# A decoder layer on one core: cross-attention's transposes go from TensorE to the DMA queue, its output projection a quarter later

## The chip, the core and the metric

The kernel is one program on one core of a Trainium2 chip. The metric is the device time of one execution in microseconds (us), lower is better. The numbers compared are medians of several executions.

## The reference

Three blocks follow one another over `x` of 4 x 2048 x 512, each with a residual and a layer normalisation: a self-attention sum, cross-attention, and a feed-forward block with 16-bit and 8-bit rounding. The change touches the second only. With 16 heads of 32, 154 keys and a bias for each head, query and key, it is

```
q, k, v = split_heads(x1), split_heads(ctx), split_heads(ctx)      # 4 x 16 x (2048 or 154) x 32
weights = softmax((q @ k.T + bias) / sqrt(32))                     # bias 1 x 16 x 2048 x 154
combined = merge_heads(weights @ v)                                # 4 x 2048 x 512
x2 = layernorm(x1 + combined @ w_out)
```

## The kernel before

`cross_attention_stage` cuts the queries into 16 units of 512 tokens (the four batches in turn at one position, then the next position: four units are a span, `s`, and the unit's batch is `b`). A unit has four quarters. Quarter `q` = 4n + i does several things side by side, each for another tile: with 128 tokens a tile, with four heads a group. Every engine has its own `quarter` function that lists its work in order, and `at(n, i, off)` (for SP and POOL `span_at`) says for which tile or group: `off` quarters ahead of q or behind it. Engines wait for each other by counting semaphores alone.

The steps, with the offset in quarters before the change:

- SP loads the tile's x1 (`load_x1`, +4). ACT rounds it to f16 as `q16` (`token_half`, +5); the same pair of x1 and q16 gives the f16 stack: the rounded q twice (`stack_halves`, +5) and, from POOL, the rest that rounding lost (`low_half`, +4). A head of the stack has 97 columns: high, high, low, and one for minus its maximum.
- PE transposes q16 into PSUM (`transpose_heads`, line 1161, 4 transposes of 128x128), ACT copies it to `q_heads` (line 977). PE multiplies it with the keys and adds the bias rows (`max_pair`, +4, 16 matmuls of 308 columns), and DVE takes each head's maximum into the stack (`maximum`, line 1041).
- PE transposes the stack, 16 heads in two halves (`transpose_stack`, line 1192, +4 and +3), ACT copies it to `qs` (line 986).
- `logits` (+0): 5 steps for the group's four heads, keys on the partitions. DVE adds the bias (`add_bias`, line 1054), ACT takes the exponential (`weights`, line 996). `values` (-1) are 20 products in f32, `normalise` (-1, -2) divides by the sum.
- The combined group is split into f16 high (ACT, `combined_high`, -2) and low (POOL, `combined_low`, -2), transposed by PE (`transpose_combined`, line 1249, 8 transposes, -3) and copied by ACT to `combT` (line 1013).
- `project` (-6): 12 matmuls of 512 columns for one tile, then DVE's `residual` (-6), POOL's `reciprocal_root` and `finish` (-7), with the store, and DVE's `magnitude` (-8).

All transposes on PE share one bank of PSUM, `ps_t16`, so each waits until ACT has copied the one before. Inside a PE quarter there are eight slots k: in each `max_pair`, in the first five `logits`, 2 or 3 of `values`, in the odd ones a quarter of `project`; the transposes stand in slots 0, 2, 4 and 6.

SP issues all loads of the stage in one queue, in order. Keys and values of the next batch come once a unit, the bias in `bt_main` and `bt_tail` (1.25 MB for each group) four times a span: in the last three quarters of it and the first of the next. POOL loads `b_rows` (616 KB a tile slot) four times a span from its own queue: before the change at b = 2, i = 1 to 3 and b = 3, i = 0. PE, ACT and DVE loop over 8 quarters a turn, SP and POOL over 16.

The feed-forward stage already uses a DMA transpose (line 1407, `xT`): 128 x 2048 f16, 512 KB, twice for each of its 16 blocks, in a stage that loads and stores blocks of 1 MB.

Of the kernel before, what the change touches and what calls it, by code (L numbers as in the profile page):

```python
# [37 lines left out]
SPAD = STACK + 1  # L38
# [586 lines left out]
def cross_attention_stage(nc, x1_rows, ks_dram, kb_dram, v_main, v_tail, bias_rows, bias_main, bias_tail,  # L625
# [12 lines left out]
    with ExitStack() as ctx:  # L638
# [49 lines left out]
        ps_t = ctx.enter_context(nc.psum_tensor("ps_t", [P, 512], F32))  # L688
        ps_t16 = ps_t[:, :].bitcast(F16)
# [17 lines left out]
        qT_done = sem("qT_done")  # L707
        qT_ready = sem("qT_ready")
        mx_done = sem("mx_done")
        mx_ready = sem("mx_ready")  # L710
        st_done = sem("st_done")
        st_ready = sem("st_ready")
# [9 lines left out]
        ct_done = sem("ct_done")  # L722
        ct_ready = sem("ct_ready")
# [22 lines left out]
        def over_quarters(eng, quarter):  # L746


            for q in range(-5, 16):
# [5 lines left out]
            for q in range(QUARTERS - 8, QUARTERS + 9):  # L755
                quarter(q // 4, q % 4, (q // 4) % 2)

        def over_spans(eng, quarter):

            for q in range(-5, 16):  # L760
                quarter(q // 16, q // 4 % 4, q % 4)
# [4 lines left out]
            for q in range(QUARTERS - 16, QUARTERS + 9):  # L766
                quarter(q // 16, q // 4 % 4, q % 4)
# [13 lines left out]
        def _(sp):  # L781
            def load_x1(s, b, t):
# [9 lines left out]
            def load_residual(s, b, t):  # L792
# [3 lines left out]
                if not (isinstance(s, int) and tile < 2):  # L796
                    sp.wait_ge(y_ready, tile - 1)
                first_tile = 4 * s if isinstance(s, int) else sp.snap(4 * s)
                sp.dma_start(xres[:, t % 2], x1_rows[b].rearrange("(n p) d -> n p d", p=P)[
                    bass.ds(first_tile + t, 1)].rearrange("n p d -> p (n d)")).then_inc(xres_in[t % 2], 16)  # L800
# [31 lines left out]
            def quarter(s, b, i):  # L832
                n = 4 * s + b if isinstance(s, int) else sp.snap(4 * s + b)
                if isinstance(s, int) and n < 0:
# [21 lines left out]
                if not (isinstance(s, int) and s == UNITS // BATCH - 1) and b == BATCH - 1 and i >= 1:  # L856
                    sp.wait_ge(biased, 5 * (4 * n + i))
                    load_bias(s + 1 if isinstance(s, int) else sp.snap(s + 1), i - 1)
# [4 lines left out]
            over_spans(sp, quarter)  # L863

        @block.gpsimd
        def _(pool):
# [7 lines left out]
            def low_half(s, b, t):  # L874
# [4 lines left out]
                if not (isinstance(tile, int) and tile < 2):  # L879
                    pool.wait_ge(st_done, 2 * (tile - 1))  # L880
# [4 lines left out]
            def combined_low(s, b, g):  # L885
# [4 lines left out]
                if not (isinstance(group, int) and group == 0):  # L890
                    pool.wait_ge(ct_done, group)
                pool.tensor_tensor(comb_lo[:], comb[:], comb_hi[:], ALU.subtract).then_inc(comb_split, 1)  # L892
# [54 lines left out]
        def _(act):  # L947
            def token_half(nu, t):
# [5 lines left out]
                if not (isinstance(tile, int) and tile < 2):  # L954
                    act.wait_ge(qT_done, tile - 1)
# [3 lines left out]
            def stack_halves(nu, t):  # L959
# [4 lines left out]
                if not (isinstance(tile, int) and tile < 2):  # L964
                    act.wait_ge(st_done, 2 * (tile - 1))
# [3 lines left out]

            def copy_heads(nu, t):  # L970
                if not inside(nu, t):
                    return
                tile = 4 * nu + t
                act.wait_ge(qT_done, tile + 1)
                if not (isinstance(tile, int) and tile < 2):
                    act.wait_ge(mx_done, 8 * (tile - 1))
                act.activation(q_heads[:, t % 2], ps_t16[:, 0:DIM], ACT.Copy).then_inc(qT_ready, 1)

            def copy_stack(nu, t, eu, half):
                if not inside(nu, t):  # L980
                    return
                tile = 4 * nu + t
                act.wait_ge(st_done, 2 * tile + half + 1)
                if not (isinstance(nu, int) and nu < 2):
                    act.wait_ge(lg_done, 20 * (nu - 1))
                act.activation(qs[:, eu, 8 * half:8 * half + 8, t * P:(t + 1) * P],  # L986
                               ps_t16[0:STACK, :].rearrange("p (h t) -> p h t", t=P), ACT.Copy).then_inc(st_ready, 1)
# [10 lines left out]
            def combined_high(nu, g):  # L998
# [4 lines left out]
                if not (isinstance(group, int) and group == 0):  # L1003
                    act.wait_ge(ct_done, group)
                act.activation(comb_hi[:], comb[:], ACT.Copy).then_inc(comb_high, 1)  # L1005

            def copy_combined(nu, g, eu):
                if not inside(nu, g):
                    return
                act.wait_ge(ct_done, 4 * nu + g + 1)  # L1010
                if not (isinstance(nu, int) and nu < 2):
                    act.wait_ge(w_done, 4 * (nu - 1))
# [1016 lines left out]
```

## Time and profile before

| | |
|---|---|
| Median of 3 runs | 2423.58 us (2409.52 to 2452.31) |
| The profiled execution | 2424.86 us |
| Its span, first to last instruction | 2423.3 us |
| PE busy | 2182.9 us, 90% |
| DVE busy | 1762.9 us, 73% |
| ACT busy | 1235.8 us, 51% |
| POOL busy | 819.8 us, 34% |
| Mean granted TensorE clock | 0.948 of full speed |
| Mean moved by the DMA engines | 168 GB/s |

Cross-attention lies between about 565 and 1425 us of the span. A time "busy" counts an engine's instructions only; a matmul's end is modelled, so that matmuls that follow one another overlap on paper, and the distance between starts tells more than their lengths.

### The profile page before, as it was taken

What the parts mean: (1) busy time and instruction counts of PE and PEld (TensorE: products, weight loads), DVE (VectorE), ACT (ScalarE), POOL (GpSimd) and SP (SyncE); (2) the same over time, 40 slices, a digit from 0 to 9 for tenths busy, and PEclk for the clock granted to TensorE, in tenths of its full rate; (3) what the DMA queues carried; (4) which work ended last, traced back from release to release, by engine and by line L of the source; (5) the groups of instructions that cost most, each with busy time, mean ns of one, the idle gap of its engine ahead of it and who ended that gap; (6) DMA issues with size and microseconds to landing.
All of it is one profiled execution on the core that took longest, in us unless ns stands there. A gap on an engine that the chain in (4) does not pass through costs nothing. (4 is left out here: it accounts for less than half of the span.)

```text
span 2423.3 us, 40289 instructions
## 1 busy us (share of the span) xinstructions
PE 2182.9 (90%) x13184; PEld 1238.5 (51%) x13184; DVE 1762.9 (73%) x3344; ACT 1235.8 (51%) x1714; POOL 819.8 (34%) x819
## 2 busy tenths in 40 slices
PE   7998999973999999999899937899999959999998
PEld 3444444431777777777677713334444424444443
DVE  5768687853787878687778835886666468888885
ACT  1444444443776766576567504344444455555551
POOL 2212222221144445344445444123222214433442
PEclk9999999996999999899989978999999979999999
DMA  6334332228437338334723136777888746666662
GB/s 219 119 103 144 116 130 103 102 81 185 131 95 186 126 109 173 125 102 102 198 96 105 57 133 214 266 231 256 266 274 268 282 157 232 229 224 226 231 228 84
DMA packets 219008, 406.52 MB, mean 168 GB/s; under 512 B 111526, under 2 KB 111814, under 8 KB 200416
## 3 DMA queue, kind: packets, MB, share of 16 engines
q1 hardware_dynamic: 154800, 244.18, 32.8%
q0 software_dynamic: 64048, 160.28, 20.0%
q8 instruction: 91, 1.49, 0.3%
q14 instruction: 69, 0.57, 0.1%
HBM read 259.00 MB, written 138.73 MB: 164 GB/s over the span
## 5 line engine op out<-in xcount | busy, mean ns | idle before, releaser
L1680 PE MATMUL ps_h<-xT,w 128*128 128x512 f16 x2048 | 453.1, 384 | 22.0 <-ACT h L1511 12.2
L1920 PE MATMUL ps<-w,g_hi 128*128 128x512 f16 x1024 | 389.7, 381 | 28.3 <-DVE g_lo L1858 28.3
L1920 PE MATMUL ps<-w,g_lo 128*128 128x512 f16 x1024 | 389.6, 380 | 0.0
L1041 DVE TENSOR_REDUCE stack<-ps_m 128x2 f16<-128x308 f32 x512 | 244.7, 480 | 133.8 <-PE ps_m L1178 109.8
L1680 PEld LDWEIGHTS ps_h<-xT,w 128*128 128x128 f16 x2048 | 201.1, 99 | 268.2 <-issue 19.3
L1511 ACT ACTIVATE h<-ps_h,b_in_sb,col_scale 128x512 f32<-128x512 f32 x256 | 198.0, 778 | 261.3 <-PE ps_h L1680 230.1
L1236 PEld LDWEIGHTS ps_o<-vm,pT 128*128 128x128 f32 x2048 | 292.0, 198 | 12.9
L1236 PE MATMUL ps_o<-vm,pT 128*128 128x33 f32 x2048 | 278.5, 261 | 0.0
L1587 DVE TENSOR_REDUCE amax_t<-h 128x1 f32<-128x2048 f32 x64 | 146.2, 2284 | 128.7 <-ACT h L1511 128.1
L996 ACT ACTIVATE pT<-logit 128x512 f32<-128x512 f32 x320 | 198.8, 624 | 71.3 <-DVE logit L1054 70.6
L1806 ACT ACTIVATE g_hi<-g 128x2048 f16<-128x2048 f32 x64 | 122.2, 1909 | 176.1 <-DVE g L1849 153.0
L297 ACT ACTIVATE raw<-ps_proj 128x512 bf16<-128x512 f32 x128 | 76.4, 597 | 249.9 <-PE ps_proj L563 249.9
L892 POOL TENSOR_TENSOR comb_lo<-comb,comb_hi 128x512 f16<-128x512 f32 x64 | 74.2, 1160 | 380.7 <-ACT comb_hi L1005 380.7
L1773 POOL TENSOR_TENSOR rstd<-vare,minus_half 128x1 f32<-128x1 f32 x64 | 132.1, 2064 | 189.2 <-DVE vare L1876 189.2
L1176 PE MATMUL ps_m<-kb,q_heads 128*128 128x308 f16 x512 | 156.4, 306 | 32.1 <-DMA b_rows<-bias_rows 13.4
L1920 PEld LDWEIGHTS ps<-w,g_hi 128*128 128x128 f16 x1024 | 100.5, 98 | 151.9 <-DVE g_lo L1858 30.6
L1054 DVE TENSOR_TENSOR logit<-ps_l,bt_main 128x512 f32<-128x512 f32 x256 | 173.8, 680 | 1.6 <-PE ps_l L1214 1.6
L1920 PEld LDWEIGHTS ps<-w,g_lo 128*128 128x128 f16 x1024 | 100.5, 98 | 121.1 <-issue 1.4
L1264 PE MATMUL ps_w<-wo_hi,combT 128*128 128x512 f16 x512 | 156.8, 389 | 5.1 <-DVE y L1082 3.1
L1178 PE MATMUL ps_m<-b_rows,ident_h 128*128 128x308 f16 x512 | 156.1, 305 | 0.0
L563 PE MATMUL ps_proj<-x_hi,w_hi 128*128 128x512 f16 x512 | 136.3, 390 | 17.2 <-DVE x_lo L383 17.2
L986 ACT ACTIVATE qs<-ps_t 97x1024 f16<-97x1024 f16 x128 | 129.7, 1013 | 40.5 <-PE ps_t L1192 39.9
(180 smaller groups left out, 4149.1 us busy)
## 6 DMA issues: line engine op xcount, KB each, us to landing
hidden<-h POOLq DMA_DIRECT2D x64, 1024.0 KB, 6.0
hT<-hidden SPq DMA_DIRECT2D x64, 1024.0 KB, 6.3
xc<-x_cols SPq DMA_DIRECT2D x16, 1024.0 KB, 5.3
xr<-x_rows SPq DMA_DIRECT2D x16, 1024.0 KB, 5.7
x_rows<-x POOLq DMA_DIRECT2D x16, 1024.0 KB, 4.8
x1t<-x_rows SPq DMA_DIRECT2D x64, 256.0 KB, 5.2
bt_main<-bias_main SPq DMA_DIRECT2D x16, 1024.0 KB, 7.6
xres<-x_rows SPq DMA_DIRECT2D x64, 256.0 KB, 3.6
```

What stands on the lines that cost most here:

```text
L563: mm = pe.matmul(ps_proj[job % 2][:], w[:, m, c, o * P:(o + 1) * P], x_[:, j % 2, c, :], start=(s == 0), stop=(s == len(terms) - 1))
L996: act.activation(pT[:, g % 2, k, :], logit[:, (g + k) % 4], ACT.Exp, scale=SCALE).then_inc(exp_done, 1)
L1041: dve.tensor_reduce(stack[:, t % 2, 2 * k:2 * k + 2, 3 * HD], ps_m[k % 2][:, 0:2 * KEYS].rearrange("p (h k) -> p h k", h=2), AX.X, ALU.max ...
L1054: dve.tensor_tensor(logit[:, (g + k) % 4], ps_l[(5 * g + k) % 2][:], bias, ALU.add).then_inc(biased, 1)
L1176: pe.matmul(out, q_heads[:, t % 2, (k // 2) * P:(k // 2 + 1) * P], kb[:, eu, 2 * k * KEYS:(2 * k + 2) * KEYS], start=True, stop=False)
L1178: pe.matmul(out, ident_h[:], b_rows[:, t, 2 * k:2 * k + 2, :], start=False, stop=True).then_inc(mx_done, 1)
L1236: mm = pe.matmul(ps_o[c][:, base + h * VW:base + (h + 1) * VW], pT[:, g % 2, part, tok], vm[:, eu, 4 * g + h, :], start=False, stop=(part ...
L1264: mm = pe.matmul(ps_w[:], combT[:, eu, a, c, t * P:(t + 1) * P], w[:, c, :], start=(c == 0 and a == 0 and w is wo_hi), stop=(c == KC - 1 a ...
L1511: act.activation(h[:, f // 4, f % 4, :], ps_h[f % 4][:], ACT.Gelu, bias=b_in_sb[:, f:f + 1], scale=col_scale[:, f:f + 1]).then_inc(h_ready, 1)
L1587: dve.tensor_reduce(amax_t[:], h[:, g].rearrange("p c t -> p (c t)"), AX.X, ALU.max, apply_absolute_value=True).then_inc(h_max, 1)
L1680: mm = pe.matmul(ps_h[f % 4][:], w1[:, c, f * P:(f + 1) * P], xT[:, e, a, :, c, :], start=(a == 0 and c == 0), stop=(a == 1 and c == KC - 1))
L1920: mm = pe.matmul(ps[t][:], g[:, e, f, t * P:(t + 1) * P], w2[:, f, :], start=(f == 0 and a == 0), stop=(f == FC - 1 and a == 1))
```

## The change

The three transposes are issued by SP as DMA transposes, straight into `q_heads`, `qs` and `combT`; the 28 transposes on PE and the four copies on ACT in each quarter go, and with them the PSUM bank `ps_t`. A head in the stack is padded from 98 to 128 columns, so that one DMA transposes 16 blocks; `qs` has 128 rows, of which `logits` uses 97. The two halves of the combined heads lie in one double-buffered `comb_parts`. The offsets move: `load_x1` +4 to +7, `token_half` +5 to +7, `stack_halves` +5 to +6, `low_half` +4 to +6, `max_pair` and `maximum` +4 to +5, `project` and `residual` -6 to -7, `finish` -7 to -8, `magnitude` -8 to -9. The rows of `b_rows` are loaded in all four quarters of b = 2. The loops run from quarter -8 and a quarter longer, and SP's is written out in full, without a loop on the chip.

```
@@ buffers
-        stack = sb("stack", [P, 2, HEADS, SPAD], F16)
+        stack = sb("stack", [P, 2, HEADS, P], F16)
-        qs = sb("qs", [STACK, 2, HEADS, BLK], F16)
+        qs = sb("qs", [P, 2, HEADS, BLK], F16)
-        comb_hi = sb("comb_hi", [P, 2, 2, P], F16)
-        comb_lo = sb("comb_lo", [P, 2, 2, P], F16)
-        combT = sb("combT", [P, 2, 2, KC, BLK], F16)
+        comb_parts = sb("comb_parts", [P, 2, 2, 4, P], F16)
+        combT = sb("combT", [P, 2, KC, 2, BLK], F16)
@@ sync (SP)
+            def turn_heads(s, b, t):
...
+                sp.wait_ge(q16_ready, tile + 1)
+                if tile >= 2:
+                    sp.wait_ge(mx_done, 8 * (tile - 1))
+                sp.dma_start_transpose(q_heads[:, t % 2].rearrange("p (c r) -> p c r", r=P),
+                                       q16[:, t % 2]).then_inc(qT_in[t % 2], 16)
+
+            def turn_stack(s, b, t):
...
+                sp.wait_ge(mx_ready, 8 * (tile + 1))
+                sp.wait_ge(high_ready, tile + 1)
+                sp.wait_ge(low_ready, tile + 1)
+                if n >= 2:
+                    sp.wait_ge(lg_done, 20 * (n - 1))
+                sp.dma_start_transpose(qs[:, n % 2, :, t * P:(t + 1) * P],
+                                       stack[:, t % 2].rearrange("p h d -> p (h d)")).then_inc(st_in[t % 2], 16)
+
+            def turn_combined(s, b, g):
...
+                sp.wait_ge(comb_split, 4 * n + g + 1)
+                if n >= 2:
+                    sp.wait_ge(w_done, 4 * (n - 1))
+                sp.dma_start_transpose(combT[:, n % 2, g].rearrange("p a (t r) -> p (a t) r", r=P),
+                                       comb_parts[:, g % 2].rearrange("p a t d -> p (a t d)")).then_inc(ct_in[g % 2], 16)
@@ SP's quarter
-                load_x1(*span_at(s, b, i, 4))
-                load_residual(*span_at(s, b, i, -6))
+                turn_heads(*span_at(s, b, i, 6))
+                turn_stack(*span_at(s, b, i, 4))
+                if 4 * n + i >= -3:
+                    load_x1(*span_at(s, b, i, 7))
+                if n < 0:
+                    return
+                turn_combined(*span_at(s, b, i, -3))
+                load_residual(*span_at(s, b, i, -7))
...
-            over_spans(sp, quarter)
+            for q in range(-8, QUARTERS + 10):
+                quarter(q // 16, q // 4 % 4, q % 4)
@@ POOL's quarter
-                low_half(*span_at(s, b, i, 4))
                 combined_low(*span_at(s, b, i, -2))
-                reciprocal_root(*span_at(s, b, i, -7))
-                finish(*span_at(s, b, i, -7))
+                reciprocal_root(*span_at(s, b, i, -8))
+                finish(*span_at(s, b, i, -8))
+                low_half(*span_at(s, b, i, 6))
...
-                elif b == 2 and i >= 1:
-                    pool.wait_ge(mx_done, 8 * (4 * (n + 1) + i))
-                    load_rows(s + 1, i - 1)
-                elif b == 3 and i == 0:
-                    pool.wait_ge(mx_done, 32 * (n + 1))
-                    load_rows(s + 1, 3)
+                elif b == 2:
+                    pool.wait_ge(mx_done, 8 * (4 * (n + 1) + i + 1))
+                    load_rows(s + 1, i)
@@ ACT: stack_halves (tile >= 2)
-                    act.wait_ge(st_done, 2 * (tile - 1))
+                    act.wait_ge(st_in[t % 2], 16 * (2 * nu + t // 2))
@@ ACT's quarter
-                copy_combined(*at(n, i, -3), (e + (i - 3) // 4) % 2)
                 weights(n, i, 0)
                 weights(n, i, 1)
-                copy_stack(*at(n, i, 3), (e + (i + 3) // 4) % 2, 1)
                 weights(n, i, 2)
                 combined_high(*at(n, i, -2))
                 weights(n, i, 3)
-                token_half(*at(n, i, 5))
-                copy_stack(n + 1, i, 1 - e, 0)
+                stack_halves(*at(n, i, 6))
                 weights(n, i, 4)
-                copy_heads(*at(n, i, 5))
-                stack_halves(*at(n, i, 5))
+                token_half(*at(n, i, 7))
@@ PE: logits and project
-                    pe.wait_ge(st_ready, 8 * n + 7)
+                    pe.wait_ge(st_in[0], 32 * (n + 1))
+                    pe.wait_ge(st_in[1], 32 * (n + 1))
...
-                    pe.wait_ge(ct_ready, 4 * (nu + 1))
+                    pe.wait_ge(ct_in[0], 32 * (nu + 1))
+                    pe.wait_ge(ct_in[1], 32 * (nu + 1))
@@ PE's quarter
-                tile = (*at(n, i, -6), (e + (i - 6) // 4) % 2)
+                tile = (*at(n, i, -7), (e + (i - 7) // 4) % 2)
                 for k in range(8):
-                    max_pair(n + 1, i, 1 - e, k)
+                    max_pair(*at(n, i, 5), (e + (i + 5) // 4) % 2, k)
...
-                        transpose_combined(*at(n, i, -3), last_use)
-                        transpose_stack(*at(n, i, 3), 1,
-                                        (ct_ready, q - 2) if inside(*at(n, i, -3)) else (qT_ready, q + 5))
-                        transpose_stack(n + 1, i, 0, (st_ready, 2 * q + 8) if inside(*at(n, i, 3)) else (qT_ready, 1))
-                        transpose_heads(*at(n, i, 5))
```

## Rows read from the trace of the kernel before

**Rows 1.** Windows over cross-attention: length, busy time (instructions) by engine, clock, DMA share, GB/s.

```profile
565.70:609.05 43.35, 19.58 (x148) 10.35 (x149) 15.25 (x35) 18.03 (x27) 10.41 (x9) 0.72 1.09 236
609.05:795.62 186.57, 175.75 (x1550) 140.52 (x1549) 146.51 (x337) 131.75 (x205) 70.48 (x70) 0.95 0.51 137
795.62:1003.92 208.30, 196.65 (x1669) 151.78 (x1668) 162.47 (x385) 135.69 (x209) 96.92 (x100) 0.95 0.51 141
1003.92:1215.55 211.63, 200.03 (x1664) 154.11 (x1664) 162.77 (x385) 135.47 (x208) 96.89 (x100) 0.93 0.47 130
1215.55:1382.00 166.45, 165.76 (x1426) 129.99 (x1426) 136.35 (x330) 112.96 (x173) 80.07 (x85) 0.97 0.25 84
1382.00:1424.70 42.70, 30.58 (x205) 19.12 (x204) 26.51 (x73) 8.77 (x12) 31.90 (x37) 0.98 0.26 87
```

**Rows 2.** Windows over single quarters (from one `bt_tail` add of DVE to the next).

```profile
853.71:865.19 11.48, 11.48 (x105) 9.10 (x103) 10.04 (x25) 8.42 (x14) 5.76 (x6) 1.00 0.44 154
...
917.85:929.39 11.54, 11.54 (x105) 9.10 (x104) 9.95 (x26) 8.45 (x13) 6.96 (x8) 1.00 0.78 128
929.39:942.41 13.02, 12.16 (x108) 9.16 (x105) 11.65 (x26) 8.45 (x13) 7.67 (x8) 1.00 0.87 173
...
953.95:969.72 15.77, 12.36 (x93) 9.02 (x92) 9.92 (x26) 7.54 (x12) 6.48 (x7) 0.86 1.17 310
...
985.36:1003.92 18.56, 15.33 (x108) 10.84 (x105) 10.15 (x25) 8.51 (x14) 5.76 (x6) 0.79 0.49 166
1003.92:1019.74 15.82, 15.67 (x104) 11.97 (x104) 10.11 (x26) 8.56 (x13) 5.75 (x6) 0.71 0.22 67
```

**Rows 3.** Timeline of PE in one quarter: start, length, line, how many.

```profile
901.32 0.39 PE L1161 MATMUL ps_t<-ident_h,q 128*128 128x128 f16 x4
901.54 0.29 PE L1176 MATMUL ps_m<-kb,q_heads 128*128 128x308 f16 x1
...
904.20 0.39 PE L1249 MATMUL ps_t<-ident_h,comb_hi 128*128 128x128 f16 x4
...
904.65 0.29 PE L1176 MATMUL ps_m<-kb,q_heads 128*128 128x308 f16 x1
...
907.48 0.63 PE L1192 MATMUL ps_t<-ident_h,stack 128*97 128x128 f16 x8
907.95 0.29 PE L1176 MATMUL ps_m<-kb,q_heads 128*128 128x308 f16 x1
```

**Rows 4.** Waits from 640 to 1382 us: total, times, longest.

```profile
DVE stack L1041 <- PE ps_m L1178: 75.3, 144, 5.7
ACT q L957 <- DMA x1t<-x_rows: 15.4, 4, 6.2
```

**Rows 5.** Line 1407 by source, the feed-forward stage's DMA transposes: issue on SP min/median/max, and landing.

```profile
L1407 SPq DMA_TRANSPOSE xT<-x_hi x16: 1838/8844/9410, 1461.6 to 1882.6; - x16
L1407 SPq DMA_TRANSPOSE xT<-x_lo x16: 2137/6224/10310, 1463.9 to 1884.4; - x16
DMA to landing us min/median/max: 4.4/9.8/16.3
```

**Rows 6.** Window of one us in which only those transposes move data.

```profile
1531.00:1532.00 1.00, 0.00 (x0) 0.00 (x0) 0.86 (x3) 0.47 (x1) 0.00 (x0) 0.50 1.19 220
```

**Rows 7.** DMA issues from 800 to 1000 us: size, median us to landing.

```profile
x1t<-x_rows SPq DMA_DIRECT2D x16, 256.0 KB, 5.1
b_rows<-bias_rows POOLq DMA_DIRECT2D x4, 616.0 KB, 8.6
```

**Rows 8.** Timeline of ACT: two neighbouring tiles before the first logits; then two steady operations.

```profile
595.53 0.60 ACT L977 ACTIVATE q_heads<-ps_t 128x512 f16<-128x512 f16 x1 [0.56 <-PE ps_t L1161]
...
601.53 0.60 ACT L977 ACTIVATE q_heads<-ps_t 128x512 f16<-128x512 f16 x1 [0.56 <-PE ps_t L1161]
...
883.24 0.62 ACT L996 ACTIVATE pT<-logit 128x512 f32<-128x512 f32 x1
885.00 0.62 ACT L967 ACTIVATE stack<-x1t 128x512 f16<-128x512 f32 x1
```

More of the change, by code:

```diff
@@ L746, in over_quarters @@
         def over_quarters(eng, quarter):
-            for q in range(-5, 16):
+            for q in range(-8, 16):
                 quarter(q // 4, q % 4, (q // 4) % 2)
@@ L754, in over_quarters @@
                         quarter(2 * m + e, i, e)
-            for q in range(QUARTERS - 8, QUARTERS + 9):
+            for q in range(QUARTERS - 8, QUARTERS + 10):
                 quarter(q // 4, q % 4, (q // 4) % 2)
         def over_spans(eng, quarter):
-            for q in range(-5, 16):
+            for q in range(-8, 16):
                 quarter(q // 16, q // 4 % 4, q % 4)
@@ L765, in over_spans @@
                         quarter(s, b, i)
-            for q in range(QUARTERS - 16, QUARTERS + 9):
+            for q in range(QUARTERS - 16, QUARTERS + 10):
                 quarter(q // 16, q // 4 % 4, q % 4)
@@ L968, in stack_halves @@
                 act.activation(stack[:, t % 2, :, HD:2 * HD], x, ACT.Copy).then_inc(high_ready, 1)
[L970 to L987, printed above, removed]
             def weights(n, g, k):
@@ L1095, in _ @@
             dve.tensor_copy(ident_h[:], ident_f[:]).then_inc(ident_ready, 1)
+            dve.memset(stack[:, :, :, STACK:P], 0.0).then_inc(ident_ready, 1)
             def magnitude(nu, t):
@@ L1139, in quarter @@
                     if k == 7:
-                        residual(*at(n, i, -6))
+                        residual(*at(n, i, -7))
                     if k == 5:
@@ L1151, in _ @@
         def _(pe):
-            def transpose_heads(nu, t):
-                if not inside(nu, t):
-                    return
-                tile = 4 * nu + t
-                pe.wait_ge(q16_ready, tile + 1)
-                if not (isinstance(tile, int) and tile == 0):
-                    pe.wait_ge(st_ready, 2 * tile - 1)
-                for c in range(KC):
-                    mm = pe.transpose(ps_t16[:, c * P:(c + 1) * P], q16[:, t % 2, c * P:(c + 1) * P], ident_h[:])
-                mm.then_inc(qT_done, 1)
             def max_pair(nu, t, eu, k):
@@ L1179, in max_pair @@
                           start=False, stop=True).then_inc(mx_done, 1)
-            def transpose_stack(nu, t, half, last_use):
-                if not inside(nu, t):
-                    return
-                tile = 4 * nu + t
-                if half == 0:
-                    pe.wait_ge(high_ready, tile + 1)
-                    pe.wait_ge(low_ready, tile + 1)
-                pe.wait_ge(mx_ready, 8 * tile + 4 * half + 4)
-                pe.wait_ge(*last_use)
-                for h in range(8):
-                    mm = pe.transpose(ps_t16[0:STACK, h * P:(h + 1) * P],
-                                      stack[:, t % 2, 8 * half + h, 0:STACK], ident_h[:])
-                mm.then_inc(st_done, 1)
             def logits(n, e, g, k):
@@ L1240, in values @@
                         mm.then_inc(pv_done, 1)
-            def transpose_combined(nu, g, last_use):
-                if not inside(nu, g):
-                    return
-                pe.wait_ge(comb_split, 4 * nu + g + 1)
-                pe.wait_ge(*last_use)
-                for a, half in enumerate((comb_hi, comb_lo)):
-                    for t in range(4):
-                        mm = pe.transpose(ps_t16[:, (4 * a + t) * P:(4 * a + t + 1) * P], half[:, t // 2, t % 2, :],
-                                          ident_h[:])
-                mm.then_inc(ct_done, 1)
             def project(nu, t, eu, c):
```

88 lines of the change are left out of this document (37 added, 51 removed).

## The prediction

> **What bounds the kernel now.** I read the windows over the stage first, then single quarters, then PE's timeline in one of them, then waits and DMA. Cross-attention holds 859 us of the span, 64 quarters of logits between a lead-in of 43 us and a drain of 43 us [rows 1]. A quarter that nothing disturbs takes 11.5 us, PE is busy in all of it at a full clock, DVE for 10.04 us, and DMA for a share of 0.44 [rows 2]. So PE bounds it, and DVE is only 1.5 us behind. 16 quarters of 11.5 us would be 184 us, but the two middle spans take 208.3 and 211.6 [rows 1]: some 25 us of each go elsewhere. The single quarters show where: those with `b_rows` under way take 11.5 and 13.0 us at a DMA share of 0.78 to 0.87, the one with bias loads 15.8 at 1.17, and the ones after it 18.6 and 15.8 at a granted clock of 0.79 and 0.71, which is a mix of 2.4 and 1.2 GHz [rows 2]. Late x1 is among the causes there [rows 4].
>
> **Removed: PE's transposes.** Their cost is the distance between starts. Eight of the stack take 907.48 to 907.95, 0.47 us, twice a quarter; the eight of the combined heads 904.20 to 904.65, 0.45; the four of q16 901.32 to 901.54, 0.22 [rows 3]. That is 1.61 us of each quarter, and PE would need 9.9. But DVE has 10.04 of work, which the change leaves alone. Between PE and DVE stand two banks for the maxima and two for the logits, so DVE can't run far ahead, and some small waits stay. The bound is 10.04 below, 11.5 above; I take 10.5, nearer to the busy row, since DVE's present waits for PE (75 us in 742, 1.2 a quarter [rows 4]) come from PE being late. **A clean quarter gains 1.0 us, not 1.6.** ACT loses four copies and has slack before and after (8.42 of 11.5 [rows 2]); I cost that at nothing.
>
> **Added: DMA transposes.** In a quarter they move 128 + 512 + 256 KB (q16 512, stack 2048, combined 1024 columns of f16 on 128 partitions), 0.92 MB. While only `xT`'s transposes run, 220 GB/s go at a share above 1, that is, the engines are full [rows 6]: 4.2 us a quarter. The clean quarter's DMA work is 0.44 x 11.5 = 5.1 us at most, so 9.3 of 10.5: it fits, barely. A span has 0.51 x 208 = 106 us of it now [rows 1] and will have 106 + 67 = 173 in some 195: it fits too, if it is spread. It isn't.
>
> The Trainium skill (DMA: Bandwidth & Descriptors, "Latency and other measured facts") gives a contiguous DMA transpose 350 to 400 GB/s and says that a non-contiguous middle dimension costs about 30%. No row here has the first figure; `xT`'s target is contiguous and got 220. As an estimate by that page's 30%, the stack's transpose, whose heads lie 1 KB apart in `qs`, would take 1 us more, which would change the `b_rows` quarters below by 12 us in all and the clean ones by nothing.
>
> **The new loop.** SP issues in order: `turn_heads`, `turn_stack`, x1, `turn_combined`, the residual, then the keys, values or bias of the quarter. ACT's `stack_halves` of tile q+6 waits until the stack of q+4 has been read out, which SP issued at the start of the same quarter; behind it stand `weights` 4 and `token_half`, whose q16 the next `turn_heads` wants, and behind that is the next `turn_stack`. So a quarter can't be shorter than: the stack's issue to landing, plus two halves of 0.62, one exponential of 0.62 and one token half of about 0.62 [rows 8], plus SP's issue of the heads (a quarter of the 1.84 that 512 KB cost it [rows 5], 0.46) and their own 0.6 us of DMA. With the shortest landing, 4.4 us [rows 5], that is 7.9; with the median of 9.8, which was measured beside 1 MB stores, 13.3. In a clean quarter the ring holds little else, and x1 lands in 5.1 [rows 7] where it could be some 3; I take 4.4 + 2 = 6.4 and get 9.9, under DVE's 10.5. This is the step with the least room.
>
> **Quarters with b_rows** (12 of them, b = 2 in three spans; all now in a row). Their DMA share of 0.78 to 0.87 is 9.0 to 11.3 us of work [rows 2]; with 4.2 more it is 13.2 to 15.5. The rows aren't wanted for three quarters, so some of it can slip into b = 3, but their packets come from POOL's queue between those of the transposes and slow the stack's. I take 13.2 against 12.3 now: 12 x 0.9 = +11. Bounds: 10.5 (-22) and 15.5 (+38).
>
> **Quarters with bias, and after** (12). Bias loads stand behind the transposes in SP's queue, x1 has less than a quarter to arrive instead of two, so the late x1 stays. What shrinks is PE's work at a low clock: 1.6 of 11.5 is 14%, of 15.8 it is 2.2. I take -1.6 each, -19. Bounds: -3 and +2 each, -36 and +24.
>
> **Clean quarters.** The first six have no projection and are bound otherwise (I give them nothing); 58 - 24 = 34 remain: -34. Bounds: -1.46 each (-50) and +1.8 (+61, if the loop takes 13.3).
>
> **Lead-in.** Two tiles now follow at 6.0 us [rows 8], and logits start after four tiles. They will start after five and the landing of tile 3's stack; a tile takes the loop's 7.3 (no exponential yet). Four steps of 7.3 and about 5 of landing are 34 against 25, and the first heads queue behind the first loads, during which 236 GB/s flow at a share of 1.09 [rows 1]. For that I take 6, an estimate between nothing and 15: +9 and +6, +15 in all. Bounds 0 and +30.
>
> **Drain.** The last group's transpose costs 0.45 on PE and a copy of 1.02 now, and by DMA some 3.5 to landing (4.4 for twice as much, less half its 2.4 of transfer, plus issue); the quarter added behind holds only a projection: +4. Bounds 0 and +8. SP's three issues are 1.84 us for 512 KB [rows 5], so 3.2 for the quarter's 896 KB, and fit into 10.5 as long as the ring takes them. The padding's one memset and the merging of the combined halves lie on no chain, and POOL has 5.76 of 11.5 busy [rows 2], so that its later `low_half` fits.
>
> **Sum:** -34 + 11 - 19 + 15 + 4 = -23 us. Against the profiled execution of 2424.9 (1.6 us over its span) that is 2402. The median, 2423.6, lies 1.3 under that execution; I leave the number at 2402.
>
> **Rivals.**
>
> A. The forecast, chance 0.44: 2360 to 2450 with its own bounds.
>
> B. DMA hides everything, DVE is the bound throughout. For it: the mean share after, 173 in 195, is under 1, and the stalls by late x1 might be absorbed by the deeper pipeline. Against it: SP's order puts x1 behind 0.64 MB. Clean quarters -1.3 x 34, `b_rows` -1.8 x 12, bias -2.5 x 12, +11 at the ends: -85, 2340. Chance 0.27.
>
> C. The loop decides: the stack's landing takes more than 7 us in ordinary quarters, from where the loop passes 10.5. For it: the median landing of 9.8; SP was held 8.8 us by one issue [rows 5], so its queue itself stalls when the ring is full. Against it: those stand behind 1 MB loads and beside 1 MB stores, here 256 KB is usual. At a landing of 8.8 the quarter is 12.3: +0.8 x 34 = +27, `b_rows` at 15.5 +38, bias 0, ends +25: +90, 2515. Chance 0.27.
>
> D. The transposes don't overlap at all: each of the three waits out a landing of 4.4 one after another, 13.2 us a quarter, 1.7 more in 58 quarters and 25 at the ends: 2549. Rows 5 and 6 speak against it, since hi and lo of `xT` are both issued before the first lands. The Trainium skill (VectorE: DVE Perf Modes, "The three transpose paths") has a 128x128 block at 1309 ns by DMA against 390 on TensorE; 28 in a row would be 37 us a quarter by that. The row has 220 GB/s, 0.15 us for a block of 32 KB, and excludes it. Chance 0.02.
>
> **Numbers.** A measurement of this kernel can tell about 2% from no change: 48 us, so faster is under 2375, slower over 2472. A gives 0.03 faster, 0.40 same, 0.01 slower; B 0.22 and 0.05; C 0.04 same and 0.23 slower; D slower. Together 0.25, 0.49, 0.26. The range is 2335 to 2500: it leaves out half of C, D and the far end of B.
>
> **What would show it.** Right: clean quarters of 10.4 to 10.7 us with DVE busy for about 10 and PE idle in short pieces; quarters with b = 2 at 12.5 to 14 with a DMA share near 1; the stack's landing at 6 to 7 us, longer in those; first logits some 15 us later. Wrong: ACT's `stack` (line of `stack_halves`) waiting for the DMA transpose in clean quarters means C; PE at a lower clock in clean quarters, because it now waits briefly each time, would spoil A and B alike and is in no row here, since DVE-bound quarters with projection don't occur.

## The result, and the profile after

The changed kernel is slower, by 1.4%. Its median is 2461.28 us (4 runs, 2452.13 to 2478.65) against 2430.22 for the kernel before on the same chip (4 runs, 2409.52 to 2452.31): a ratio of 1.0142 [1.0101, 1.0183]. The forecast was 2402. The profiled executions, 2463.74 and 2424.86 us, lie 38.9 apart, and the 38.9 are what has to be found.

From the page of the kernel after: busy time, the granted clock in 40 slices, and the queues (packets, MB, share of 16 engines' span).

```profile
span 2462.2 us, 35958 instructions
PE 2154.9 (88%) x11368; PEld 1165.3 (47%) x11392; DVE 1775.3 (72%) x3345; ACT 1019.0 (41%) x1458; POOL 805.7 (33%) x819
...
PEclk9999999985558998989889977999999989999999
...
DMA packets 454485, 464.55 MB, mean 189 GB/s; under 512 B 347046, under 2 KB 347334, under 8 KB 435936
...
q1 hardware_dynamic: 390320, 302.92, 46.9%
```

ACT lost 217 us of work. PE lost only 28 us of busy time though 1792 transposes (28 x 64) left it: three slices of the stage stand at 5 tenths, that is, at a granted clock of 1.2 GHz, and there the rest of PE's work takes longer.

The windows over the stage after, with the columns of [rows 1]: lead-in, three spans, the last span, drain.

```profile
561.80:624.96 63.16, 23.44 (x87) 6.32 (x88) 20.25 (x44) 9.71 (x18) 11.07 (x10) 0.55 0.99 194
624.96:836.81 211.85, 195.64 (x1108) 146.95 (x1107) 144.43 (x330) 82.42 (x144) 67.23 (x67) 0.72 0.88 186
836.81:1043.35 206.54, 180.88 (x1216) 126.99 (x1216) 164.99 (x386) 81.02 (x144) 96.55 (x100) 0.91 0.97 209
1043.35:1251.62 208.27, 182.41 (x1216) 127.90 (x1216) 167.11 (x385) 80.80 (x144) 96.55 (x100) 0.89 0.90 201
1251.62:1410.98 159.36, 152.88 (x1071) 108.98 (x1072) 138.95 (x329) 66.92 (x119) 80.16 (x85) 0.95 0.69 165
1410.98:1456.00 45.02, 31.04 (x168) 17.08 (x166) 27.61 (x76) 4.68 (x8) 34.68 (x40) 0.92 0.42 120
```

The first span lost 25 us to [rows 1], at a clock of 0.72 against 0.95. The two middle spans gained 2 and 3, the last 7. The DMA share of the middle spans went from 0.51 and 0.47 to 0.97 and 0.90.

The single quarters of the kernel after, against [rows 2]: one before the projection starts; the first with b = 2, at whose end POOL issues `b_rows`, and the one behind it; one behind the boundary of a loop; two clean ones; one of the last span.

```profile
689.35:703.32 13.97, 13.97 (x65) 11.47 (x65) 8.18 (x18) 5.22 (x9) 2.27 (x2) 0.50 0.66 160
734.12:744.12 10.00, 10.00 (x78) 7.41 (x76) 8.98 (x23) 5.01 (x9) 5.04 (x6) 1.00 0.84 193
744.12:759.68 15.56, 11.54 (x80) 7.64 (x77) 9.59 (x25) 5.12 (x9) 8.86 (x9) 0.87 1.16 213
1043.35:1060.39 17.04, 16.90 (x73) 11.86 (x74) 10.04 (x25) 5.12 (x9) 5.74 (x6) 0.53 0.61 182
1071.71:1083.26 11.55, 10.40 (x76) 7.29 (x76) 11.02 (x25) 5.01 (x9) 5.74 (x6) 1.00 0.65 152
1083.26:1094.57 11.31, 10.40 (x76) 7.29 (x76) 10.59 (x26) 5.01 (x9) 5.74 (x6) 1.00 0.63 147
1290.58:1301.54 10.96, 10.40 (x76) 7.29 (x76) 10.24 (x25) 5.01 (x9) 5.74 (x6) 1.00 0.77 156
```

And the kernel before: the quarter that answers to the first of them (no projection either), ahead of it a stretch of its second quarter in which its clock was low too.

```profile
617.00:627.00 10.00, 10.00 (x56) 8.67 (x54) 5.02 (x9) 4.31 (x7) 1.16 (x1) 0.50 0.69 229
650.81:660.24 9.43, 9.10 (x93) 8.06 (x94) 7.54 (x18) 8.23 (x14) 2.27 (x2) 1.00 0.24 93
```

Cut at the same places in both kernels (from one `bt_tail` add to the next), the difference falls into these groups of quarters. The forecast's terms stand beside them.

| | before | after | difference | forecast |
|---|---|---|---|---|
| start to first logits | 609.05 | 624.96 | +15.9 | +15 |
| first eight quarters | 85.4 | 109.2 | **+23.8** | 0 (for six) |
| 12 of b = 2, `b_rows` | 147.9 | 162.3 | +14.5 | +11 |
| 12 with bias, and after | 185.0 | 165.4 | -19.6 | -19 |
| 28 clean | 314.6 | 307.0 | **-7.6** | -34 (for 34) |
| 3 at the end of a turn of the loop of PE, ACT and DVE | 42.1 | 42.2 | +0.1 | (in the 34) |
| last logits to the last running maximum | 41.6 | 45.0 | +3.4 | +4 |
| the stages behind | 997.7 | 1006.2 | +8.5 | |

They add up to 39.0. Four groups came near their forecast; the two bold ones did not. The last five of the 28 clean quarters, in which the maxima run out (8.5 to 11.7 us each before), give 5.3 of the 7.6. The other 23 went from 11.55 to 11.45 us on average: they gained next to nothing. The line by line answers of the kernel after, for the DMA transposes of `qs`, of `q_heads` and of `combT` (durations on SP in ns min/median/max, then landing):

```profile
L795 SPq DMA_TRANSPOSE qs<-stack x64: 1503/2076/8321, 594.8 to 1374.8; - x64
...
DMA to landing us min/median/max: 4.3/5.7/15.2
```

```profile
L782 SPq DMA_TRANSPOSE q_heads<-q x64: 1189/1197/4434, 574.2 to 1352.4; - x64
...
DMA to landing us min/median/max: 2.4/2.5/13.9
```

```profile
L805 SPq DMA_TRANSPOSE combT<-comb_parts x64: 1237/1242/3562, 663.6 to 1428.8; - x64
...
DMA to landing us min/median/max: 3.0/4.0/9.8
```

The stack lands in a median of 5.7 us, under the 7 from which rival C would decide. And five of the waits of the kernel after from 640 to 1410 us, which answer to [rows 4]:

```profile
PEld ps_m L1167 <- DVE stack L1042: 69.1, 44, 8.1
DVE stack L1042 <- PE ps_m L1169: 64.5, 82, 2.2
PE ps_m L1167 <- DVE stack L1042: 46.9, 40, 7.6
...
ACT stack L999 <- DMA qs<-stack: 34.4, 14, 5.2
...
ACT q L989 <- DMA x1t<-x_rows: 1.1, 1, 1.1
```

PE now waits for DVE's maxima: DVE is the bound in the clean quarters, as forecast. But it has more to do there, 10.59 to 11.02 us busy against 10.04 in [rows 2], though its work was left alone. This is the extra in a clean quarter of the kernel after, in the timeline (start, length, engine, line):

```profile
1093.06 1.20 DVE L1116 TENSOR_TENSOR amax_run<-amax_run,amax_t 128x1 f32<-128x1 f32 x1
1093.07 1.16 POOL L913 TENSOR_TENSOR stack<-x1t,q 128x512 f16<-128x512 f32 x1
```

and the same operation of the kernel before, which meets only the last 0.09 us of `low_half`:

```profile
852.01 1.17 POOL L881 TENSOR_TENSOR stack<-x1t,q 128x512 f16<-128x512 f32 x1
...
853.09 0.16 DVE L1113 TENSOR_TENSOR amax_run<-amax_run,amax_t 128x1 f32<-128x1 f32 x1
```

`amax_run`, one number a partition, took 0.16 us there and 1.20 where it lies wholly beside POOL's `low_half`. All 64 of them took 21.8 us before, 10 of them over 0.5 us each, and 39.7 us after, 29 over 0.5; 20 of these 29 lie in the 23 full clean quarters.

So the theory that I took to the chip was: (1) in the first quarters the clock doesn't come back up, since PE's transposes, which kept PE at the full clock there, are gone; (2) in the clean ones `low_half`, moved behind `finish`, holds up DVE's running maximum. The rival for both was that the DMA transposes themselves cost the time.

### The profile page after: what moved, and what is told of

The parts are those of the page before. It is cut to its first block and busy times, and to the rows that moved or that the text cites. A ratio compares the mean times of both kernels' runs of the same rounds, so it can differ in the third digit from the quotient of the medians.

```text
span 2462.2 us, 35958 instructions
## 1 busy us (share of the span) xinstructions
PE 2154.9 (88%) x11368; PEld 1165.3 (47%) x11392; DVE 1775.3 (72%) x3345; ACT 1019.0 (41%) x1458; POOL 805.7 (33%) x819
## 5 line engine op out<-in xcount | busy, mean ns | idle before, releaser
L1629 PE MATMUL ps_h<-xT,w 128*128 128x512 f16 x2048 | 453.3, 384 | 32.4 <-ACT h L1460 17.8
L1211 PEld LDWEIGHTS ps_o<-vm,pT 128*128 128x128 f32 x2048 | 322.4, 216 | 15.3
L1211 PE MATMUL ps_o<-vm,pT 128*128 128x33 f32 x2048 | 302.2, 275 | 0.0
L1167 PE MATMUL ps_m<-kb,q_heads 128*128 128x308 f16 x512 | 172.3, 337 | 98.2 <-DVE stack L1042 55.9
L924 POOL TENSOR_TENSOR comb_parts<-comb,comb_parts 128x512 f16<-128x512 f32 x64 | 74.0, 1157 | 402.2 <-ACT comb_parts L1018 402.2
L1722 POOL TENSOR_TENSOR rstd<-vare,minus_half 128x1 f32<-128x1 f32 x64 | 119.6, 1868 | 191.9 <-DVE vare L1825 191.9
L1229 PE MATMUL ps_w<-wo_hi,combT 128*128 128x512 f16 x512 | 162.3, 400 | 15.9 <-DVE y L1083 15.9
L1169 PE MATMUL ps_m<-b_rows,ident_h 128*128 128x308 f16 x512 | 172.2, 336 | 0.0
L1167 PEld LDWEIGHTS ps_m<-kb,q_heads 128*128 128x128 f16 x512 | 80.7, 158 | 160.5 <-DVE stack L1042 92.7
L1807 DVE TENSOR_TENSOR g_lo<-g,g_hi 128x2048 f16<-128x2048 f32 x64 | 146.5, 2289 | 4.8 <-ACT g_hi L1755 4.5
```

Source lines behind the costliest of these rows:

```text
L1167: pe.matmul(out, q_heads[:, t % 2, (k // 2) * P:(k // 2 + 1) * P], kb[:, eu, 2 * k * KEYS:(2 * k + 2) * KEYS], start=True, stop=False)
L1169: pe.matmul(out, ident_h[:], b_rows[:, t, 2 * k:2 * k + 2, :], start=False, stop=True).then_inc(mx_done, 1)
L1211: mm = pe.matmul(ps_o[c][:, base + h * VW:base + (h + 1) * VW], pT[:, g % 2, part, tok], vm[:, eu, 4 * g + h, :], start=False, stop=(part ...
L1229: mm = pe.matmul(ps_w[:], combT[:, eu, c, a, t * P:(t + 1) * P], w[:, c, :], start=(c == 0 and a == 0 and w is wo_hi), stop=(c == KC - 1 a ...
L1629: mm = pe.matmul(ps_h[f % 4][:], w1[:, c, f * P:(f + 1) * P], xT[:, e, a, :, c, :], start=(a == 0 and c == 0), stop=(a == 1 and c == KC - 1))
L1807: dve.tensor_tensor(g_lo[:, e, 4 * g:4 * g + 4, :], g32[:, g], g_hi[:, e, 4 * g:4 * g + 4, :], ALU.subtract).then_inc(lo_ready, 1)
```

## The experiments

All are the kernel after with one edit, unless said. Ratios are to the kernel before on the same chip.

**fill_lead** gives PE 28 transposes a quarter back, of the identity into a spare bank, in the lead-in and the first seven quarters alone.

```
+        ps_f = ctx.enter_context(nc.psum_tensor("ps_f", [P, 512], F32))
...
+                    if k % 2 == 0 and isinstance(n, int) and 4 * n + i < 7:
+                        for f in range(7):
+                            pe.transpose(ps_f[:, :].bitcast(F16)[:, f * P:(f + 1) * P], ident_h[:], ident_h[:])
```

> The changed kernel, and in every quarter before the first projection (up to quarter 6) PE also does 28 transposes of the identity into an unused PSUM bank, as many as the kernel before had there. Theory 1 (without its transposes, PE's mix of maxima, logits and small f32 products can't bring the granted clock back from 0.5 once it has fallen): the clock is 1.0 from quarter 1 or 2 on, quarters 1 to 6 take 8.5 to 10 us instead of 11.8 to 16.2, and the kernel takes 25 to 40 us less than the changed one (about 2425 us). Theory 2 (the clock stays low because of the gaps and late DMA in the lead-in): still 0.5 until the projection starts, quarters get longer by 3 us at that clock, and the kernel is 10 to 20 us slower than the changed one (about 2475).

2451.05 us, 1.0105 [1.0041, 1.0169]. Its windows over four quarters before the projection:

```profile
660.40:674.77 14.37, 14.23 (x80) 12.04 (x80) 7.95 (x18) 5.23 (x9) 2.27 (x2) 0.50 0.22 51
674.77:684.34 9.57, 9.57 (x93) 8.54 (x94) 7.66 (x18) 5.01 (x9) 2.28 (x2) 0.94 0.89 178
684.34:693.28 8.94, 8.94 (x93) 8.02 (x94) 7.66 (x17) 5.01 (x9) 2.28 (x2) 1.00 0.95 181
693.28:701.89 8.61, 8.61 (x86) 7.61 (x87) 7.57 (x17) 5.12 (x9) 2.28 (x2) 1.00 0.89 203
```

With 28 more instructions a quarter it takes 9 us in place of 13.97: the clock returns to 2.4 GHz, though only from the fifth quarter on. The first eight quarters are 89.8 us against 109.2. The DMA share stands at 0.9 in the last three of these windows, so at 9 us the transposes by DMA don't hold the quarter. The total fell by less than the 25 to 40 us of the expectation, and its interval overlaps that of the change itself (1.0101 to 1.0183): what is shown is the quarters, not the total.

**one_input** writes the running maximum with one tensor input and one scalar operand.

```
-  dve.tensor_tensor(amax_run[:], amax_run[:], amax_t[:, t % 2:t % 2 + 1], ALU.max)
+  dve.tensor_scalar(amax_run[:], amax_run[:], amax_t[:, t % 2:t % 2 + 1], None, ALU.max)
```

> The changed kernel with DVE's update of the running maximum as a tensor_scalar with a pointer scalar instead of a tensor_tensor with two SBUF inputs; the same values. Theory 1 (DVE bounds the clean quarter and its 0.84 to 1.2 us in that 128x1 operation are a block by POOL's two-input stack subtraction that now runs beside it): the operation takes about 0.16 us, clean quarters fall from 11.3 to 10.3 to 10.6 us, 25 to 45 us in all (about 2425). Theory 2 (it waits for something else, or DVE has slack): quarters stay at 11.0 to 11.3, no difference.

2449.99 us, 1.0082 [1.0044, 1.012]. The operation by source, and a clean quarter:

```profile
L1116 DVE TENSOR_SCALAR amax_run<-amax_run,amax_t x64: 212/214/216, 760.1 to 1427.1; 128x1 f32<-128x1 f32 x64
```

```profile
1055.06:1065.32 10.26, 10.11 (x77) 7.29 (x76) 9.70 (x25) 5.01 (x9) 5.38 (x7) 1.00 0.70 164
```

It never takes over 0.216 us, and the 28 clean quarters take 290.3 us in place of 307.0. All 16.7 us come from the 23 full ones, 10.72 us on average in place of 11.45; the forecast had missed 20.4 in the 28 (7.6 for 28). Here too the interval of the total overlaps that of the change. The Trainium skill (SBUF — State Buffer, "SBUF: two separate sides") has DVE and GpSimd share one pair of ports that whichever comes first holds for its whole instruction, and counts a DVE operation with two SBUF inputs, beside a GpSimd operation that reads SBUF, among those that need it. Both runs agree on who is held: 1.20 us beside 1.16 with two inputs, 0.21 with one. On who came first they don't settle it: by the records some of the 29 start up to 0.46 us ahead of `low_half` and are held all the same, until 0.02 us behind its end (the longest 1.65 us), and POOL's records are rough.

**tiny** puts an ordinary DMA of 8 bytes a partition in the place of each DMA transpose, so what `q_heads`, `qs` and `combT` hold isn't the transpose; waits and order stay.

```
-                sp.dma_start_transpose(qs[:, n % 2, :, t * P:(t + 1) * P],
-                                       stack[:, t % 2].rearrange("p h d -> p (h d)")).then_inc(st_in[t % 2], 16)
+                sp.dma_start(qs[:, n % 2, 0, t * P:t * P + 4], stack[:, t % 2, 0, 0:4]).then_inc(st_in[t % 2], 16)
```

> The changed kernel with each of the three DMA transposes replaced by an ordinary DMA of 8 bytes a partition on the same queue with the same waits and semaphores; q_heads, qs and combT are set to zero once at the start and stay so (4 KB of them aside). It shows what the transposes' data and issue cost. Theory 1 (they cost the quarters with b_rows and bias, and the stretches at a low clock that follow each stall): quarters 9 to 16 and 24 to 31 fall to about 11, the kernel to some 2380. Theory 2 (the loss is in the lead-in's clock alone): quarters 1 to 7 stay at 14 us and the kernel is within 15 us of the changed one, about 2450.

2404.28 us, 0.9908 [0.9875, 0.9942]: the transposes' data and issue cost 57 us in all, so the rival is worth more than either part of the theory. By groups: 14.6 us up to the first logits, 13 of the first eight quarters, 21 of the `b_rows` ones (11.78 each), 16.5 of the bias ones, 5 of the clean ones, 1.5 of the three with a turn. That is 71 up to the last logits; the rest of the kernel took 11.5 us longer than after. Yet a quarter before the projection stands at the low clock here too, with a DMA share of 0.24. Its second quarter, ahead of it, has the same 65 instructions on PE at 2.4 GHz:

```profile
616.73:624.06 7.33, 7.26 (x65) 6.22 (x65) 6.89 (x16) 4.51 (x9) 1.16 (x1) 1.00 1.01 374
650.26:664.23 13.97, 13.97 (x65) 11.47 (x65) 8.18 (x17) 5.23 (x9) 2.27 (x2) 0.50 0.24 64
```

This is the same 13.97 as after, 6.6 us more than the same instructions took at the full clock. What DMA decides there is when the clock falls: `tiny` ran its first two quarters at 1.0.

**fill_before0** has the same filling as fill_lead, but in the lead-in's quarters only (`4 * n + i < 0`). It asks whether the gaps of the lead-in set the clock of the quarters behind it.

> The changed kernel with the 28 idle transposes a quarter only before quarter 0, none from quarter 0 on. Theory 1 (once the clock is down, PE's mix of maxima, logits and small f32 products can't lift it, whatever came before): after the stall in quarter 2 the clock falls to 0.5 and stays there until the projection starts in quarter 7, with quarters 3 to 6 at 12 to 14 us. Theory 2 (the gaps of the lead-in are the cause, and PE kept busy there is enough): quarters 3 to 6 at 8.5 to 10 us and a clock of 1.0.

One run, 2464.6 us. The clock is 0.50 again from the third quarter to the seventh:

```profile
688.03:702.00 13.97, 13.97 (x65) 11.48 (x65) 8.18 (x17) 5.23 (x9) 2.27 (x2) 0.50 0.68 160
```

The first eight quarters take 109.2 us, as after. So it is the work of those quarters themselves that leaves the clock at 1.2 GHz, not what PE did in the lead-in.

**norows** loads `b_rows` once and not for the later spans (their bias is the first span's); **early_res** puts the residual's load a quarter earlier, ahead of the combined transpose.

```
-                elif b == 2:
-                    pool.wait_ge(mx_done, 8 * (4 * (n + 1) + i + 1))
-                    load_rows(s + 1, i)
```

> The changed kernel without the reloads of b_rows after the first span (POOL issues none in b = 2; the maxima use the first span's rows). Theory 1 (b_rows' small packets between those of the transposes slow the stack's landing, ACT and DVE wait for it, and the clock falls after that): the quarters of b = 2 fall from 13 to 14.5 us to 11.3, 12 of them, and with the low clocks after them 30 to 45 us in all (about 2425). Theory 2 (the transposes' own load or SP's order is the cause): less than 12 us.

2440.02 us, 1.0058 [1.0033, 1.0083]. That is some 20 us less than the change, clear of its interval, if under the 30 to 45 expected. The quarters of b = 2 fall from 162.3 to 138.7 us and look like clean ones:

```profile
948.41:959.73 11.32, 10.40 (x76) 7.29 (x76) 10.79 (x26) 5.01 (x9) 5.75 (x6) 1.00 0.65 151
```

```
+                load_residual(*span_at(s, b, i, -6))
                 turn_combined(*span_at(s, b, i, -3))
-                load_residual(*span_at(s, b, i, -7))
```

> The changed kernel with one load moved: SP issues the residual's load one quarter earlier (offset -6) and ahead of turn_combined. Theory 1 (in the quarters with b_rows DVE waits at the residual for xres, whose load stands behind two DMA transposes that hold SP's queue, and PE waits for DVE): those waits of up to 5.8 us go, the 12 quarters with b = 2 fall by 1 to 3 us each, 15 to 30 us in all with the low clocks after them (about 2435). Theory 2 (the quarter is held by the stack's landing, which ACT waits for, and the residual only shows it): under 8 us.

2485.58 us where before had 2458.93, 1.0122 [1.0036, 1.0208]. Its b = 2 quarters take 155.8 us, 6.5 less. In the total nothing can be seen, since its interval holds that of the change itself; the 15 to 30 us of the expectation don't show.

**unroll** writes PE's, ACT's and DVE's quarters out in full, as SP's are.

```
-            with eng.Fori(2, UNITS // 2 - 1) as m:
...
+            for q in range(-8, QUARTERS + 10):
```

> The changed kernel with the loops of PE, ACT and DVE written out in full. Theory 1 (at the end of each turn of 8 quarters the engines stand still for some 4 us with no wait, and the granted clock is low for most of the quarter after): the five quarters of 15.4 to 18.1 us fall to about 11.3 and the ones after them from 13.6 to 17.0 to 11.3: 30 to 45 us (about 2422). Theory 2 (instructions then come too slowly from memory, beside DMA that is already near full): pauses appear elsewhere, the kernel is no faster or slower by 20 us or more.

2471.32 us against 2458.93, 1.0071 [1.0027, 1.0114]. The three quarters at a turn of the loop fall from 42.2 to 33.6 us. They aren't alike: two take 15.40 and 15.81 us and fall to 11.31 and 11.32, while the third, where the loop is left, took 10.95 and stays there. Those with bias (which hold further turns) fall from 165.4 to 143.1. The clean ones get 10.5 us longer (317.5); three of them now take 13.9 to 14.8.

**combo** joins fill_lead, one_input and early_res, and moves ACT's `stack_halves`, of the steady quarters, behind the last exponential. **combo_unroll** is this with the loops written out.

```
-                stack_halves(*at(n, i, 6))
+                if isinstance(n, int) and n < 0:
+                    stack_halves(*at(n, i, 6))
                 weights(n, i, 4)
+                if not (isinstance(n, int) and n < 0):
+                    stack_halves(*at(n, i, 6))
```

> The changed kernel with four small edits together: 28 idle transposes a quarter on PE up to quarter 6, the running maximum as a tensor_scalar, the residual's load one quarter earlier and ahead of turn_combined, and ACT's stack_halves after token_half instead of ahead of weights 4. If the parts add up: 12 (lead-in) + 12 (running maximum) + 10 to 25 (residual) + 0 to 10 (stack_halves) less than 2461, that is 2405 to 2425, at or under the kernel before. If one stall only takes the place of another: 2430 to 2440.

> The four edits and the loops of PE, ACT and DVE written out in full. With theory 1 of the unrolled loops: 30 to 45 us less than the four edits alone, about 2375, clearly under the kernel before. With theory 2: no gain over the four edits.

combo: 2435.24 us against 2458.93, 0.9906 [0.9861, 0.9952]; combo_unroll: 2425.85, 0.9857 [0.9772, 0.9941]. In the first, the 23 full clean quarters average 10.42 us:

```profile
1047.91:1058.16 10.25, 10.10 (x77) 7.29 (x76) 9.71 (x25) 5.13 (x9) 5.34 (x7) 1.00 0.85 224
```

**control** is the kernel before, once more, to see how far the stages behind differ from one execution to the next.

> The kernel before, unchanged, for its profile on the same chip as the others of this call. Theory 1 (what differs between profiles outside the changed stage is the chip or the execution, not the change): its time from the last logits to the end of the span lies as far above 1039 us as that of the next kernel does. Theory 2 (the change slows the feed-forward stage too): it has 1039 us, and the others 1050 to 1090.

2423.7 us. From the last running maximum to the end it has 1008.2 us, where the first profile of the same kernel had 997.7: two executions of one kernel differ there by more than the +8.5 of the table. So these needn't be the change's; that none of them is isn't shown, as the 10.5 of control lie in one block of the feed-forward stage (37.5 us in place of 27.6) that the kernel after passes in 28.0. Its stage has 83.6, 145.4 and 180.8 us in the first eight, `b_rows` and bias quarters, within 4.2 of the table's "before".

**four_edits** is combo with ACT's order left alone and `w_out` loaded two quarters earlier.

```
-                if isinstance(s, int) and n == 0 and i == 2:
+                if isinstance(s, int) and n == 0 and i == 0:
```

> The changed kernel with the 28 idle transposes on PE up to quarter 6, the running maximum as a tensor_scalar, the residual's load one quarter earlier ahead of turn_combined, and w_out loaded in quarter 0 instead of 2; ACT's order as in the changed kernel. Theory 1 (stack_halves behind token_half gave nothing: it frees x1 later, and ACT waited 65 us for x1 in that variant): as fast as the combination with it, ratio to the kernel before 0.985 to 0.995, with few waits of ACT for x1. Theory 2 (ACT's wait for the stack's transpose was a real limit): some 10 us slower than that combination, ratio 0.995 to 1.0.

2416.06 us against 2424.51, 0.9956 [0.9925, 0.9987]. ACT's wait for the stack stands in its waits, where combo's has instead the wait for x1 that comes next in its order:

```profile
ACT stack L1000 <- DMA qs<-stack: 64.2, 25, 12.0
```

```profile
ACT q L990 <- DMA x1t<-x_rows: 65.2, 25, 11.4
```

Bias quarters take 164.1 us against combo's 153.6, clean ones 281.7 against 283.4. So the wait of rival C exists once the other limits are gone. That it is what the bias quarters pay isn't shown, since four_edits and combo differ in the load of `w_out` as well and ran on two chips. In the total the two intervals overlap (0.9925 to 0.9952), and whether ACT's order is worth anything there isn't settled.

**combo_unroll5** is combo_unroll over more runs, to size the best version.

> The kernel combo_unroll once more, for a narrower interval. Its loops are written out, so that no quarter carries the pause at a loop's end; its median lay at 0.9857 of the kernel before, 0.977 to 0.994. Theory 1 (written-out loops give 5 us or more beyond the four edits): ratio 0.984 to 0.989. Theory 2 (what they take from the loops' ends comes back as waits for b_rows quarters and x1): 0.989 to 0.993, no different from combo.

2408.09 us against 2434.17 (12 and 17 runs), 0.9875 [0.9833, 0.9917]. It beats both kernels, the one before by 1.25%. What the written-out loops add to combo isn't shown, since combo's interval (0.9861 to 0.9952) overlaps this one.

## Why the prediction was wrong

**The step that failed first** is "The first six have no projection and are bound otherwise (I give them nothing)". Given nothing, they cost 17.8 us, and with the next two, which the forecast had among its clean ones, 23.8, more than half of the 38.9. The step treated the taking of work from PE as free wherever PE wasn't credited for it. In these quarters of the kernel before, PE was busy for 9.10 of 9.43 us at 2.4 GHz; after, it is busy for all of 13.97 at 1.2 GHz, and the clock is low from 633 to 728 us. The kernel before fell to 1.2 GHz there too, at 617 us, but was back some 10 us later. The projection comes in from 720 us on, and from 728 us the clock is back (10.00 us at 1.00 in the quarter from 734). fill_lead shows that 28 transposes a quarter bring it back, fill_before0 that the lead-in's filling doesn't, and tiny that it stays low without the DMA transposes. My last lines named PE at a lower clock as what would spoil A and B, but looked for it in the clean quarters, where it isn't (1.00), and gave it neither a price nor a chance.

**The second** is the size of the clean quarter, 10.5 us; the full ones took 11.45. The bound was named rightly: DVE, with PE idle in short pieces. Its work was taken from [rows 2] as 10.04 and "the change leaves [it] alone", but the change moves POOL's `low_half` behind `finish`. I costed that by POOL's free time, and not by what it meets: DVE's running maximum, in 20 of the 23 full clean quarters. With one_input the 28 quarters take 24.3 us less than before, 0.87 each where the forecast had 1.0, so the term would have been nearly right but for this.

**What held.** The lead-in (+15.9 for +15) held with its mechanism: SP issues the heads of neighbouring tiles at 603.82, 611.23 and 618.58, a step of 7.4 for the 7.3 forecast, and tiny, without the transposes' data, reaches the first logits 14.6 us earlier. The drain (+3.4 for +4) and the b = 2 quarters (13.53 each for 13.2) held in size, the latter as a mean of quarters from 10.0 to 15.9 us. For the b = 2 quarters the split is shown in part: norows gives 23.6 us back, tiny 21, early_res 6.5, so they are short of DMA, in bursts, while the span's mean share is under 1. The quarter from 744 us has 1.16, and in it SP is held for 8.32 us by one issue:

```profile
754.57 8.32 SPq L795 DMA_TRANSPOSE qs<-stack  x1
```

**What came out by luck** are the bias quarters, -19.6 for -19. The forecast gave each of the 12 a gain of 1.6 for PE's work at a low clock, and said that the late x1 stays. It didn't stay: ACT waits 1.1 us for x1 in all, where it waited 15.4 [rows 4]. The gain isn't spread either: the first bias quarter of each span, 11.31 us in the second span where [rows 2] have 15.77, gives 16.8 us of the 19.6 in three quarters. The ones beside a turn of the loop gained at most 2.1 or got longer:

```profile
1003.80:1015.11 11.31, 10.39 (x76) 7.29 (x76) 10.71 (x25) 5.01 (x9) 5.74 (x6) 1.00 1.03 283
1026.93:1043.35 16.42, 10.40 (x76) 7.29 (x76) 10.66 (x26) 5.01 (x9) 5.74 (x6) 0.97 1.10 283
```

Two figures of mine were off without deciding anything: SP's issue of the heads was taken as a quarter of 1.84 us, 0.46, and it is 1.19 at the least; SP's three issues were taken as 3.2 us a quarter, and their medians add up to 4.5.

**The rivals.** B (DMA hides everything, 2340) is refuted: tiny is what B assumes, it is 57 us faster, and even it took 2404. C (the loop decides) isn't what happened, though its sign was right: the stack lands in 5.7, and ACT's waits for it are 34.4 us in all from 640 us on. D is excluded, 11.3 us a quarter against its 13.2. None of my rivals held the measured mechanism, and those on the slower side stood at 2515 and 2549.

What stays open: why two quarters at a turn of the loop take over 15 us in both kernels. unroll shows that the turn is the cause, not which part of it. Which property of PE's work keeps the clock low, when it is busy all the time, isn't shown either. And what the edits give in the stage isn't all found in the total: up to the last logits fill_lead is 25.7 us shorter than after and one_input 28.4, while their medians are 10 and 11 lower. From there to the end the profiles differ widely, 1039 us before, 1051 after, 1065 and 1069 in these two, 1085 in early_res, most of it in single blocks of the feed-forward stage that take 33 to 41 us in place of 27.6. Control has one of these too; their cause is open.

## What to carry to other kernels

Taking matmuls off TensorE can cost time where what is left doesn't bring it back to the full clock, as here in the first quarters: look for stretches in which it has other work than elsewhere, and price them at the low clock too. When a GpSimd operation is moved, look at which VectorE operation it will now lie beside, down to those of one column. And judge added DMA by the fullest quarter, not by the mean of the span.

## What the runs showed of the hardware

- A PE that is busy throughout can stay at 1.2 GHz: 13.97 of 13.97 us at a granted clock of 0.50, some 95 us long (633 to 728), with matmuls of 308 and 512 columns in f16 and of 33 and 132 in f32; with seven transposes more in every other slot it is at 1.00 within two quarters.
- A 128x1 `tensor_tensor` of DVE with both inputs in SBUF took up to 1.65 us beside a POOL operation of 1.17 us, 0.16 alone; it ended 0.02 us behind POOL's. With one input and a scalar operand it took 0.21 and was never held.
- A DMA transpose costs SP at least 1.19 us to issue, even for 128 KB; 128, 256 and 512 KB land in 2.4, 3.0 and 4.3 us at the least.
- The stack's transpose, whose heads lie apart in the target, landed in 4.3 us at the least; the same 512 KB into a contiguous target did in 4.4 [rows 5]. The 30% that the prediction quoted from the Trainium skill (DMA: Bandwidth & Descriptors, "Latency and other measured facts") aren't seen in these.
- A turn of the loop of PE, ACT and DVE costs 4.1 and 4.5 us in the quarter at whose end it stands (15.40 and 15.81 to 11.31 and 11.32, by unroll); leaving the loop costs nothing there (10.95 and 10.97).
